# Another placing of side stages in a transformer kernel, with tables of zero products on TensorE

## What is computed

```python
h = layernorm(x) * (1 + ca) + sa
x = x + ga * causal_attention_32(h)          # block 0: one head, width 32
h = layernorm(x) * (1 + cb) + sb
x = x + gb * top1_experts(h)                 # block 0: gating over 128 scores, 8 experts
h = layernorm(x) * (1 + ca) + sa
x = x + ga * attention_16_heads(h)           # block 1: 16 heads of width 8, over all 1024 tokens
h = layernorm(x) * (1 + cb) + sb
x = x + gb * (h @ W1[b].T + b1[b]) @ W2[b].T + b2[b])   # block 1: one linear pair for each batch
```

## Time and profile before

| | us |
|---|---|
| median of 3 runs | 1739.2 (1736.26 to 1743.79) |
| profiled execution, its own time | 1754.4 |
| its span, first to last instruction | 1753.0 |
| TensorE (PE) busy | 1621.5 (92%) |
| VectorE (DVE) busy | 1495.7 (85%) |
| ScalarE (ACT) busy | 1370.7 (78%) |
| GpSimd (POOL) busy | 678.4 (39%) |
| mean granted TensorE clock | 0.962 of full speed |

### The profile page before, as it was taken

One profiled execution on the slowest core, in us unless ns is written; L12 is line 12 of the kernel. 1 busy time (PEld: TensorE's weight loads), 2 busy tenths in 40 slices (PEclk: granted clock), 3 DMA queues, 4 the chain that ended last, 5 costly groups with the idle time before them and its releaser, 6 DMA issues.

```text
span 1753.0 us, 55013 instructions
## 1 busy us (share of the span) xinstructions
PE 1621.5 (92%) x23302; PEld 670.6 (38%) x23313; DVE 1495.7 (85%) x2256; ACT 1370.7 (78%) x1934; POOL 678.4 (39%) x1085
## 2 busy tenths in 40 slices
PE   5769899999999999999999999999999999988998
PEld 2543343334334443334334343334334342223224
DVE  4649988999889998999889998999889998899853
ACT  4442678987899878987899878987899877777774
POOL 2421335445534365444534365345544362002010
PEclk9998999999999999999999999999999998899888
DMA  2120101112210311112210311112110311011100
GB/s 72 51 65 25 61 31 51 35 47 70 79 35 24 90 55 51 36 45 68 72 46 20 94 55 51 36 42 71 54 53 17 95 45 62 22 33 47 41 17 23
DMA packets 83281, 87.10 MB, mean 50 GB/s; under 512 B 9452, under 2 KB 67484, under 8 KB 83036
## 3 DMA queue, kind: packets, MB, share of 16 engines
q1 hardware_dynamic: 82492, 83.07, 15.8%
q10 hardware_dynamic: 544, 0.52, 0.1%
HBM read 61.02 MB, written 21.99 MB: 47 GB/s over the span
## 4 chain that ended last, share of the span: by engine, by line
PE 59%; DVE 18%; ACT 13%; issue 6%; POOL 3%; DMA 1%; SPq 0%; ACTq 0%; POOLq 0%; DVEq 0%
PE pv_psum L798 20%; PE side_psum L526 15%; PE buffer L783 11%; DVE row_max L1335 11%; ACT p L1011 8%; PE buffer L773 6%; PE side_psum L616 2%; PE buffer L526 2%; PE side_psum L583 2%; ACT o_sb L1020 1%; DVE idx L1207 1%; DVE s L1181 1%; POOL xn_f L1371 1%; DVE st_f L1074 1%; DVE top L1201 1%
## 5 line engine op out<-in xcount | busy, mean ns | idle before, releaser
L1335 DVE TENSOR_REDUCE row_max<-buffer 128x2 f32<-128x1024 f32 x1024 | 1223.0, 1218 | 133.3 <-PE buffer L773 120.2
L1011 ACT ACTIVATE p<-buffer 128x1024 f32<-128x1024 f32 x1024 | 1044.0, 1026 | 206.1 <-PE buffer L783 193.3
L798 PE MATMUL pv_psum<-p,v 128*9 128x256 f32 x8192 | 606.9, 396 | 6.1 <-ACT o_sb L1020 2.9
L773 PE MATMUL buffer<-k_ops,q_ops 24*128 24x512 f16 x2048 | 410.7, 398 | 35.5 <-ACT p L1011 23.4
L783 PE MATMUL buffer<-q_ops,k_ops 26*128 26x512 f16 x2048 | 409.3, 397 | 20.6 <-DVE row_max L1335 18.2
L798 PEld LDWEIGHTS pv_psum<-p,v 128*9 128x9 f32 x8192 | 153.5, 90 | 251.9 <-issue 172.3
L783 PEld LDWEIGHTS buffer<-q_ops,k_ops 26*128 26x128 f16 x2048 | 96.5, 91 | 398.7 <-issue 245.5
L773 PEld LDWEIGHTS buffer<-k_ops,q_ops 24*128 24x128 f16 x2048 | 96.9, 91 | 156.3 <-ACT p L1011 119.3
L1481 POOL TENSOR_SCALAR nm_parts<-nm 128x16 f16<-128x16 f32 x64 | 19.1, 298 | 342.2 <-DVE nm L1258 342.2
L1466 POOL TENSOR_TENSOR hm<-masks,hT_f 128x1024 f32<-128x1024 bf16 x56 | 120.3, 2149 | 55.5 <-PE side_psum L526 52.3
L526 PE MATMUL side_psum<-we,hm 128*32 128x128 f32 x3648 | 122.8, 276 | 2.4 <-issue 2.4
(11 more groups left out here) (309 smaller groups left out, 1622.1 us busy)
## 6 DMA issues: line engine op xcount, KB each, us to landing
masks<-masks_rows SPq DMA_DIRECT2D x16, 1024.0 KB, 5.6
q_ops<-products SPq DMA_DIRECT2D x256, 48.0 KB
k_ops<-products SPq DMA_DIRECT2D x256, 48.0 KB
attention<-o_sb SPq DMA_DIRECT2D x248, 18.0 KB
x<-in_L_attn_inputs SPq DMA_DIRECT2D x8, 512.0 KB, 4.5
products<-q_parts SPq DMA_DIRECT2D x16, 256.0 KB, 2.3
w_sb<-in_L_ffn_W SPq DMA_DIRECT2D x16, 256.0 KB, 2.9
out<-x SPq DMA_DIRECT2D x16, 256.0 KB, 2.3
```

Of the source, the lines that this page charges most:

```text
L773: m = e.matmul(buffer[:, hh, :], q_ops[rows, slot, of, i * P:(i + 1) * P], k_ops[rows, slot, of, halves(half)[1]], start=True, stop=True)
L798: m = e.matmul(pv_psum[q:q + VW, half * QUARTER:(half + 1) * QUARTER], v1[b % 2][:, kb, 2 * hp + hh, :], p_sb[n % KEPT][:, hh, part * QUAR ...
L1011: e.activation(p_sb[n % KEPT][:, :, :], unit("exp", n)[0][:, :, :], ACT.Exp, scale=over_scale[n // (2 * PERIOD)]).then_inc(S["exp_done"], 1)
L1335: e.tensor_reduce(mx[pair % 2][:, :, i, half], unit("max", n)[0][:, :, :], axis=AX.X, op=ALU.max).then_inc(S["max_done"], 1)
```

## The change

Four things are changed; nothing that is computed for the output is.

1. `PLACES`: most stages move by a few half steps, most by one or two, some by up to 12 (of 1339 stages in the plan of half steps 644 stay where they are). The lists `ALONE`, `LAST_BESIDE` and `LAST_LINE` stay.
2. `COUNTED`, `SWITCH` and `LIGHT` get other values, so that 248 of 1024 units of `values` come in another half step. Half steps with two units are 319 (291 before), with one 386 (442), with none 321 (293).
3. `keep_busy` issues products of 256 columns, not 512. In place of `BUSY_AHEAD` the table `ZEROS_AHEAD` has 264 of them at 34 places ahead of stages of the first and last part (before: 46 of 512 at 6 places). In half steps under 0, 128 of 256 columns are spread unevenly (before: 64 of 512).
4. `zeros_beside` is new: in 70 of the half steps from 834 to 1019 it issues, behind the half step's side stages, one to three zero products (151 in all), each as four column tiles side by side over 256 columns, into the bank of the side stages. It waits until that bank's last user has read it.

```diff
-SWITCH, LIGHT = 1.2, 5.4
+SWITCH, LIGHT = 1.4, 5.7
...
 PLACES = """
--16 maxima 0, -15 nm_split 0, -10 nm 0, 0 maxima 1, 6 nm_split 1, 5 nm 1, 15 maxima 2, 12 nm_split 2, 19 nm 2, 31 maxima 3, 35 nm_split 3, 38 nm 3, 47
+-17 maxima 0, -14 nm_split 0, -10 nm 0, 0 maxima 1, 1 nm_split 1, 5 nm 1, 15 maxima 2, 14 nm_split 2, 20 nm 2, 32 maxima 3, 33 nm_split 3, 36 nm 3, 49
...
-BUSY_AHEAD = {("channels", 0, 1, 1): 12, ("channels", 0, 2, 1): 10, "steps": 4, ("channels_b", B - 1, 0): 16, ("ffn", B - 1, 0): 2, ("ffn", B - 1, 1): 2}
+ZEROS_AHEAD = {
+    "steps": 12, "channels_b 7 0": 36, "ffn 7 0": 13, "channels 0 1 1": 33, "channels 0 2 1": 23, "onehotT 0 1": 4, "scores 0 7 0": 4, "moe_a 0 2": 2,
+    "transpose_p 1 3 0": 13, "qk1 0 1 0": 8, "gates 1": 8, "transpose_p 1 4 1": 3, "moe 0 1": 8, "moe 0 4": 9, "transpose_p 1 2 0": 20, "v1 0 0": 11,
...
+ZEROS_BESIDE = {
+    -32: 2, -30: 3, -27: 2, -26: 3, -24: 4, -22: 6, -21: 3, -20: 2, -19: 1, -18: 2, -17: 10, -16: 5, -15: 1, -14: 2, -13: 6, -12: 6, -11: 5, -10: 6,
+    -9: 3, -8: 5, -7: 7, -6: 8, -5: 5, -4: 10, -3: 10, -2: 4, -1: 7, 834: 3, 837: 3, 839: 2, 841: 3, 844: 1, 846: 3, 850: 1, 851: 2, 852: 2, 854: 1,
+    859: 1, 864: 3, 867: 3, 871: 1, 872: 1, 874: 1, 877: 3, 878: 1, 881: 1, 883: 2, 884: 2, 886: 1, 891: 3, 892: 3, 893: 2, 895: 1, 898: 3, 899: 1,
...
             for n in range(count):
-                e.matmul(pv_psum[:, :], ident_bf[:, :], zero[:, :].broadcast_to([P, BANK]), start=True, stop=True)
+                e.matmul(pv_psum[:, 0:QUARTER], ident_bf[:, :], zero[:, :].broadcast_to([P, QUARTER]), start=True, stop=True)
+
+        def zeros_ahead(*stage):
+
+            count = ZEROS_AHEAD.get(" ".join(map(str, stage)), 0)
+            if count:
+                keep_busy(count)
+
+        def zeros_beside(last_side, count):
+
+            pe.wait_ge(S["side_" + last_side.by], last_side.emptied)
+            for n in range(count):
+                for q in range(0, P, COLUMN_TILE):
+                    e.matmul(side_psum[q:q + COLUMN_TILE, 0:QUARTER], ident_bf[:, q:q + COLUMN_TILE], zero[:, :].broadcast_to([P, QUARTER]), start=True, stop=True)
...
-            if h < 0:
-                keep_busy(1 if h < -LEAD else 3)
+            sides = [side[stage] for stage in plan.get(h, ()) if stage in side]
+            side_now = sides[-1] if sides else side_now
+            open_side = any(name.endswith("_a") for name, *at in plan.get(h, ()))
+            if ZEROS_BESIDE.get(h) and not open_side:
+                if h < 0:
+                    keep_busy(ZEROS_BESIDE[h])
+                else:
+                    zeros_beside(side_now, ZEROS_BESIDE[h])
```

More of the change, by code:

```diff
@@ L110 @@
 PLACES = """
--16 maxima 0, -15 nm_split 0, -10 nm 0, 0 maxima 1, 6 nm_split 1, 5 nm 1, 15 maxima 2, 12 nm_split 2, 19 nm 2, 31 maxima 3, 35 nm_split 3, 38 nm 3, 47
-maxima 4, 50 nm_split 4, 57 nm 4, 63 maxima 5, 64 nm_split 5, 70 nm 5, 80 maxima 6, 85 nm_split 6, 90 nm 6, 97 maxima 7, 93 nm_split 7, 102 nm 7, 83
-load_w12 0, 101 wout 0, 95 w2T 0, 97 wff_a 0, 98 wff 0, 116 x_bias 0, 140 sums_load 0, 142 sums 0, 146 sums_out 0, 146 sums_in 0, 144 numerators 0 0,
-151 numerators 0 1, 152 wout_mm 0 0, 154 wout_mm 0 1, 158 stats_b 0 0 0, 160 stats_b 0 0 1, 162 stats_b 0 1 0, 163 apply_b 0 0, 164 stats_b 0 1 1, 169
@@ L115 @@
[L115 to L130, removed]
@@ new lines @@
+maxima 4, 52 nm_split 4, 53 nm 4, 67 maxima 5, 68 nm_split 5, 70 nm 5, 85 maxima 6, 83 nm_split 6, 90 nm 6, 95 maxima 7, 94 nm_split 7, 100 nm 7, 80
+load_w12 0, 98 wout 0, 95 w2T 0, 97 wff_a 0, 98 wff 0, 116 x_bias 0, 134 sums_load 0, 141 sums 0, 137 sums_out 0, 146 sums_in 0, 143 numerators 0 0,
+145 numerators 0 1, 151 wout_mm 0 0, 154 wout_mm 0 1, 161 stats_b 0 0 0, 161 stats_b 0 0 1, 163 stats_b 0 1 0, 161 apply_b 0 0, 164 stats_b 0 1 1, 165
+apply_b 0 1, 168 x_wff 0, 167 channels_b 0 0, 169 ffn 0 0, 170 channels_b 0 1, 172 ffn 0 1, -207 stats 0 0 0 0, -199 stats 0 0 0 1, -195 stats 0 0 1
@@ new lines @@
+0, -193 stats 0 0 1 1, -195 apply 0 0 0, -193 apply 0 0 1, -192 channels 0 0 0, -191 g0 0 0, -190 channels 0 0 1, -188 g0 0 1, -189 v0 0, -189 later
+0, -193 gates 0, -187 scores 0 0 0, -185 softmax 0 0, -184 exp0 0 0, -185 scores 0 1 0, -183 transpose_p 0 0 0, -182 softmax 0 1, -181 exp0 0 1, -180
+scores 0 2 0, -179 transpose_p 0 1 0, -178 softmax 0 2, -182 times_v 0 0, -177 exp0 0 2, -176 scores 0 3 0, -175 transpose_p 0 2 0, -174 softmax 0 3,
+-174 times_v 0 1, -173 exp0 0 3, -166 sums0 0 0, -172 scores 0 4 0, -171 scores 0 4 1, -170 transpose_p 0 3 0, -168 transpose_p 0 3 1, -168 softmax 0
@@ new lines @@
+4, -167 times_v 0 2, -165 exp0 0 4, -165 scores 0 5 0, -164 scores 0 5 1, -163 transpose_p 0 4 0, -162 transpose_p 0 4 1, -159 softmax 0 5, -160
+times_v 0 3, -157 up 0 0, -158 exp0 0 5, -155 scores 0 6 0, -153 scores 0 6 1, -152 transpose_p 0 5 0, -151 transpose_p 0 5 1, -150 softmax 0 6, -149
+times_v 0 4, -148 exp0 0 6, -150 scores 0 7 0, -147 scores 0 7 1, -146 transpose_p 0 6 0, -145 transpose_p 0 6 1, -143 softmax 0 7, -141 times_v 0 5,
+-142 exp0 0 7, -132 sums0 0 1, -140 transpose_p 0 7 0, -139 transpose_p 0 7 1, -137 times_v 0 6, -136 times_v 0 7, -135 up 0 1, -156 stats 0 1 0 0,
@@ new lines @@
+-154 stats 0 1 0 1, -150 apply 0 1 0, -143 channels 0 1 0, -142 wg 0 0, -141 top 0 0 0, -140 top 0 0 1, -140 index 0 0 0, -140 index 0 0 1, -135
+gating 0 0 0, -137 onehot 0 0, -133 gating 0 0 1, -131 onehotT 0 0, -128 over_gating 0 0, -137 masks_out 0 0, -128 masks_load 0 0, -125 hm 0 0, -122
+hm 0 1, -121 moe_a 0 0, -120 moe 0 0, -121 hm 0 2, -116 moe_a 0 1, -115 moe 0 1, -121 hm 0 3, -112 moe_a 0 2, -111 moe 0 2, -107 moe_a 0 3, -106 moe 0
+3, -105 residual 0 0, -101 stats 0 2 0 0, -100 stats 0 2 0 1, -99 apply 0 2 0, -93 channels 0 2 0, -88 qk1 0 0 0, -69 parts 0 0 0, -91 qk1 0 1 0, -85
@@ new lines @@
+parts 0 1 0, -85 v1 0 0, -132 stats 0 1 1 0, -132 stats 0 1 1 1, -129 apply 0 1 1, -127 channels 0 1 1, -126 wg 0 1, -125 top 0 1 0, -123 top 0 1 1,
+-124 index 0 1 0, -120 index 0 1 1, -121 gating 0 1 0, -119 onehot 0 1, -116 gating 0 1 1, -117 onehotT 0 1, -102 over_gating 0 1, -119 masks_out 0 1,
+-118 masks_load 0 1, -109 hm 0 4, -107 hm 0 5, -100 moe_a 0 4, -99 moe 0 4, -97 hm 0 6, -95 moe_a 0 5, -94 moe 0 5, -88 hm 0 7, -83 moe_a 0 6, -82 moe
+0 6, -79 moe_a 0 7, -78 moe 0 7, -74 residual 0 1, -76 stats 0 2 1 0, -74 stats 0 2 1 1, -74 apply 0 2 1, -70 channels 0 2 1, -69 qk1 0 0 1, -64 parts
@@ L143, in lay_out @@
+0 0 1, -66 qk1 0 1 1, -58 parts 0 1 1, -68 v1 0 1"""
+COUNTED = {0: 2, 1: 12, 2: -0.5, 3: -2.5, 4: 11.5, 5: -6, 6: -6.5, 7: 9.5, 8: 0.5, 9: 4, 10: -6, 11: -4.5, 12: 2, 13: 8, 14: -4, 15: -6.5, 16: 6, 17: 9, 18:
[7 rows of a table added]
 def lay_out():
@@ L812, in tensor_program @@
                 early[name, *at]()
-            if (name, *at) in BUSY_AHEAD:
-                keep_busy(BUSY_AHEAD[name, *at])
+            zeros_ahead(name, *at)
             if name in stages:
                 stages[name](*at)
-        keep_busy(BUSY_AHEAD["steps"])
+        zeros_ahead("steps")
         for bank, u in before_steps.items():
@@ L820, in tensor_program @@
                 pe.wait_ge(S["side_" + u.by], u.emptied)
+        side_now = None
         for h in range(-2 * LEAD, PAIRS * UNITS + 2):
```

6 lines of the change are left out of this document (1 added, 5 removed), and 19 rows, old and new, of tables (COUNTED, ZEROS_AHEAD, ZEROS_BESIDE).

## The result

| | before | after |
|---|---|---|
| median of 13 runs each | 1736.4 (1732.6 to 1743.8) | 1745.7 (1736.3 to 1752.6) |
| profiled execution: its own time | 1754.4 | 1740.6 |
| its span; mean granted clock | 1753.0; 0.962 | 1739.3; 0.989 |

A forecast was written before the change was run, and what follows sets the result against it. VectorE was taken to bound the kernel at clock 1.00, TensorE in stretches at 0.50. 12.0 + 1.0 + 1.5 - 4.0 + 3.0 + 1.5 - 0.4 = 14.6 us less than 1739.2 gave 1724.6 us, range 1711 to 1746.

The forecast's parts named there:

- half steps 0 to 832: Eight falls of 3.4 us, worth 0 to 0.8 us each: 1.5 us less (0 to 6); moved side stages 0.
- the end: Ahead of the first `wff` product, thirteen zeros of 256 columns delay TensorE: 0.4 us more.
- 12.0 + 1.0 + 1.5: Gains at the clock: two long stretches at 0.50, two short ones (1539.5, 1631.7), and the one at 1713.6 us.
- The price of the zeros: Zeros in half steps from 834 on lengthen them, mostly those with two units of `values`: 4 us more (0 to 8).
- 0.3 to spare with one unit: At clock 1.00 TensorE has 0.3 us to spare in a half step with one unit of `values`, none with two.
- The two long stretches: From 1478.0 and 1655.5 us, at clock 0.50: zeros keep 1.00, each gives back 6.0 us, 12.0 together.
- the rival on the slow side: Half steps 839 to 983 stay at 0.50 despite the zeros, which cost TensorE 10.3 us there: 1753.9 us, chance 0.15.
- The first long fall stays: Rival: clock falls at half step 838, zeros of 839 to 854 paid at 0.50, 10.1 us lost: 1734.7 us, chance 0.22.
- The short falls: Short stretches at 0.50 at 1539.5 and 1631.7 us: five half steps each, 0.5 us each, 1.0 us less.
- The first part: Up to half step 0: higher clock and filled waits, less the cost of zeros on the chain: 3.0 us less (0 to 6).
- placing costs what the clock gives: Rival: each of 6.5 batches loses 1.5 us to late side stages, 10 us in all: 1734.6 us, chance 0.11.
- The marks: Signs of being right: clock 1.00 in half steps 838 to 856 and 966 to 984, mean 0.98, first `row_max` by 130 us.

The follow-up runs named there:

- second profile: The kernel before run once more, unchanged, against itself: profiled span 1733.1 us at a clock of 0.979; ratio of its runs 0.9994.
- first profile: The kernel before, unchanged, in the execution read for the prediction: own time 1754.4 us, span 1753.0 us, clock 0.962.
- places only: The kernel before with the new `PLACES`, `COUNTED`, `SWITCH` and `LIGHT` and the old zeros: ratio 1.0050.
- waits up to 952: The kernel before with the waits of `zeros_beside` for the side tile in half steps 834 to 952 alone, no zero products behind them: ratio 1.0027.
- zeros ahead only: The kernel before with the new zeros ahead of stages and in half steps under 0, none from half step 0 on: ratio 1.0017.
- waits that never hold: The kernel before with 70 waits in half steps on the always present identity matrix, no zero products behind them: ratio 1.0011.

## Why the prediction was wrong

The forecast was 1724.6 us, faster by 14.6; the median is 1745.7. I go by its own steps. In the table the program is cut at `row_max` of half steps 0 and 832 and at the start of the last exponentials. The last column compares with the second profile of the kernel before, which is nearer to its ordinary executions (1734.5 us, a median of 1737.3 beside it).

| part | forecast | after less the first profile | after less the second profile |
|---|---|---|---|
| up to half step 0 | -3.0 | 181.6 - 182.5 = -0.9 | 181.6 - 179.5 = +2.1 |
| half steps 0 to 832 | -1.5 | 1281.8 - 1286.5 = -4.7 | 1281.8 - 1285.6 = -3.8 |
| 832 to the last exponentials | -10.5 | 256.3 - 264.9 = -8.6 | 256.3 - 248.9 = +7.4 |
| the end | +0.4 | 19.6 - 19.1 = +0.5 | +0.5 |
| sum | -14.6 | -13.7 | +6.2 |

**The step that failed** is the first of the sums: "the runs' median is 1739.2, 15.2 lower, and I take every difference over to it unchanged". 27.4 us at 0.50 twice, and the 12 us that they were to give back, belonged to an execution that is rare (133 us at half clock, 87 in the median one); in an ordinary execution most of it wasn't there to be won, and in the second profile none of it. Its own numbers warned of it: 1754.4 lay above the highest of three runs, 1743.79, and the 15.2 us were almost the sum of what I wanted to win at the clock (12.0 + 1.0 + 1.5). I should have asked in which part of the program the 15.2 us lie, and given the case that they are these stretches a chance of its own. By it the sum would have been -14.6 + 12 + 1 + 1.5 = -0.1, no change.

**The price of the zeros** was the second error: 4 us (0 to 8) taken, 9.7 measured. The price of one group was about right, 0.4 taken and 0.45 found for three. Behind `values` three column-tiled zeros add some 0.3 us. Wrong was "0.3 to spare with one unit": TensorE's idle time stands behind the scores, where the buffers are waited for, and the zeros stand ahead of them. A part that no term had is the wait for the side tile, 1.2 us of the 9.7 with the old places. I held half steps with two units to be the dear ones (7 of some 8 us in that sum); they are 2.2 to 2.4 of the 8.1 us.

**The two long stretches.** 17 x 0.35 = 6.0 us each was a little low: 29.74 - 22.48 = 7.3 and 29.34 - 22.07 = 7.3. That zeros hold the clock was right: 0.96 and 0.94 in after, and 49 us at half clock against 99 for the same kernel without the zeros beside. Of the five profiles with these zeros in all or most of the 70 half steps none has a fall of over 3.4 us in the two stretches; of the ten without them seven have one of 13.7 to 30.7 us. So the rival on the slow side, zeros that don't hold the clock, falls; the case came out slow by a way that I didn't have. "The first long fall stays" falls too.

**The short falls and the last part.** Of the falls at 1539.5 and 1631.7 none is left; at 1706.5 one of 3.5 us is, as held possible.

**The first part.** The first `row_max` is at 128.8 us, against 131.7 in the first profile and 131.1 in the second, as forecast. But half steps -32 to 0 take 52.8 us in after and 48.4 in the second profile, with 13.7 us at half clock there against 3.4, so it is given back before half step 0. The fall behind 131 us wasn't mended. Against the second profile this part is 2.1 us longer where 3.0 less were forecast, and the zeros ahead by themselves take 4.9 us at equal clock: their price was put too low, too. Which of the 34 places takes it isn't shown.

**Half steps 0 to 832** gave more than the 1.5 us: 3.8, within the bounds. A batch takes 195.7 to 199.1 us, against 196.1 to 199.2 before. (The prediction counts eight falls from half step 0 to 832 and has three 8s among the last seven digits of the clock; the trace has nine falls, and the digits have five 8s. Neither changes its sum by more than 1 us.) The rival "placing costs what the clock gives" is right for the last part alone: places only is 1.0050, not by late stages (1.7 us at equal clock), but by time at half clock (5.0 us), which the zeros then take away again.

**The marks** that I had set (clock at 1.00 in those half steps, mean clock 0.98 or more, first `row_max` at 130 us or earlier) came true, all but to the letter, in a kernel that is slower. They tested the mechanism against one profile; none tested whether the loss was there in an ordinary run of before.

## What to carry to other kernels

Before putting a price on a repair, ask whether the execution in the profile is like the runs: when its own time lies outside theirs, find the part of the program in which it differs, and take no gain from there. Where two engines hand buffers to each other in order, idle time behind a wait is no room for fillers ahead of the work that is waited for, and a filler's wait can hold both. Judge a trade of work for clock by splitting the difference: so much by the clock, so much at equal clock.

## What the runs showed of the hardware

- The clock differs between executions of one program: 123 executions of the kernel before have spans from 1729.0 to 1757.4 us, and 0.31 us for each us at half clock tell nearly all of it (1.6 us are left).
- Most falls last 3.4 us, a good number 6.8 to 17.1. In half steps 839 to 857 and 966 to 984, with scores of 24 or 26 rows and `values` of 9 columns alone behind them, some last 23.9 to 30.7 us, though TensorE is busy 30.24 of 30.40 us. The same instructions also come through with a fall of 13.7 us (waits up to 952), of 3.4 (zeros ahead only; waits that never hold) or with none (the second profile). What decides it stays open. The Trainium skill, page "TensorE: Matmul & The Clock Gate", Part 1, says that the clock follows how busy the array is; the busy time of the rows, as these runs show again, doesn't tell that.
- Waits that never hold cost TensorE nothing that can be told (70 of them: 1.0011). 70 true ones, of which the one at half step 920 visibly holds, cost 0.5%, most of it by the clock.
- One product of 128 x 128 weights with 256 zero columns holds the queue no shorter than four column tiles of it side by side: three take 0.44 and 0.45 us. Behind `values` (column tiles too) it starts 0.11 us later than they do, 0.55 against 0.44 us after the `values`.
